# Mamba input projection of a decoder layer: batch by batch, with the softplus of batch 0 beside the projection of batch 1, and the convolution reading PSUM

## What is computed

```python
proj = hidden_states @ in_proj_w
x, z = jnp.split(proj, 2, axis=-1)
...
for k in range(K):
    xc = xc + conv_w[None, :, k:k + 1] * xp[:, :, k:k + Lq]
xc = jax.nn.silu(xc)
ssm_p = jnp.einsum('bdl,ed->ble', xc, x_proj_w)
dt_r = rmsnorm(ssm_p[..., :R], dt_ln_w)
...
dt = jnp.einsum('blr,dr->bdl', dt_r, dt_proj_w)
dt = jax.nn.softplus(dt + dt_bias[None, :, None])
...
ys = _selective_scan(xc, dt, A, Bm, Cm)
y = (ys + D_param[None, :, None] * xc) * jax.nn.silu(z)
```

## Time and profile before

| what | us |
|---|---|
| median of 3 runs | 3049.44 |
| lowest and highest run | 3047.0 and 3049.85 |
| span of the profiled execution | 3047.5 |
| VectorE, TensorE busy in it | 2393.1 and 2833.3 |
| first to last product of the input projection | 9 to 231.5 |
| softplus on VectorE | 236.9 to 318.3 |
| first scan step on VectorE | 318.24 |

### The profile page before, as it was taken

How to read it: one execution, slowest core, us unless ns; L and a number is a source line. 1 busy time by engine, 2 the same in 40 slices (tenths; PEclk the granted TensorE clock), 3 DMA queues, 4 the chain that set the end, 5 groups by cost and what they waited for, 6 DMA issues and landing times. The chain is left out here.

```text
span 3047.5 us, 35696 instructions
## 1 busy us (share of the span) xinstructions
PE 2833.3 (93%) x11958; PEld 2028.4 (67%) x11958; DVE 2393.1 (79%) x2168; ACT 1574.6 (52%) x2685; POOL 1712.8 (56%) x1035
## 2 busy tenths in 40 slices
PE   8997588888788889999999999999989999999997
PEld 7882244444222348888888888887768888887886
DVE  6558999999999977444777777765988888885677
ACT  4448555555665545213888888873433333334443
POOL 0003999999999953403888888861044444430034
PEclk9995799999999999999999999999989999999999
DMA  4228886666875645232111111215245555567654
GB/s 152 83 83 261 274 200 159 179 171 152 250 219 148 199 150 216 104 119 72 37 37 37 37 37 37 71 54 200 97 156 180 180 179 180 180 218 238 194 176 139
DMA packets 217641, 445.84 MB, mean 146 GB/s; under 512 B 33661, under 2 KB 47741, under 8 KB 215613
## 3 DMA queue, kind: packets, MB, share of 16 engines
q1 hardware_dynamic: 179742, 390.73, 41.1%
q10 hardware_dynamic: 37728, 52.96, 5.3%
HBM read 313.45 MB, written 130.15 MB: 146 GB/s over the span
## 5 line engine op out<-in xcount | busy, mean ns | idle before, releaser
L1927 POOL TENSOR_TENSOR at_p_lo<-at_p,at_p_hi 128x512 fp32r<-128x512 f32 x384 | 514.6, 1348 | 244.3 <-ACT at_p_hi L1820 236.5
L716 POOL TENSOR_TENSOR scan_dbx<-scan_u,scan_b_bc 128x1024 f32<-128x1024 f32 x256 | 596.1, 2359 | 0.0
L885 ACT ACTIVATE mamba_ps<-scan_dt,scan_a_neg 128x512 f32<-128x512 f32 (+1 forms) x512 | 332.0, 680 | 315.1 <-DVE scan_g L903 291.3
L914 DVE TENSOR_TENSOR_SCAN mamba_ps<-mamba_ps,scan_dbx 128x1024 f32<-128x1024 f32 x195 | 440.0, 2283 | 3.1 <-ACT mamba_ps L887 1.7
L1847 DVE TENSOR_REDUCE at_neg_max<-heads_ps 128x1 fp32r<-128x1536 f32 x128 | 224.9, 1757 | 134.4 <-PE heads_ps L1939 132.4
L108 PE MATMUL heads_ps<-ff_x_hi,ff_w_hi 128*128 128x512 f32 x784 | 310.0, 395 | 17.2 <-DVE ff_u L2572 6.4
L2812 POOL TENSOR_TENSOR ff_raw<-ff_raw,ff_scale 128x512 f32<-128x512 f32 x112 | 115.9, 1066 | 361.2 <-DMA ff_raw<-in_w 252.8
L109 PE MATMUL heads_ps<-ff_x_lo,ff_w_hi 128*128 128x512 f32 x784 | 308.1, 393 | 0.0
L110 PE MATMUL heads_ps<-ff_x_hi,ff_w_lo 128*128 128x512 f32 x784 | 308.1, 393 | 0.0
L1816 ACT ACTIVATE at_p<-heads_ps 128x512 f32<-128x512 f32 x384 | 228.2, 594 | 110.0 <-PE heads_ps L1963 95.8
L1820 ACT ACTIVATE at_p_hi<-at_p 128x512 fp32r<-128x512 f32 x384 | 242.8, 632 | 12.2
(11 more groups left out here) (306 smaller groups left out, 6906.8 us busy)
## 6 DMA issues: line engine op xcount, KB each, us to landing
scan_dt<-dt SPq DMA_DIRECT2D x120, 256.0 KB, 4.8
scan_u<-u SPq DMA_DIRECT2D x120, 256.0 KB, 7.6
ff_raw<-in_w SPq DMA_DIRECT2D x56, 512.0 KB, 4.6
ff_down_ar<-ac SPq DMA_DIRECT2D x98, 256.0 KB, 2.8
ff_down_hr<-hc SPq DMA_DIRECT2D x98, 256.0 KB, 2.7
ff_act_w<-in_w SPq DMA_DIRECT2D x14, 1024.0 KB, 7.6
hc<-ff_act_t SPq DMA_DIRECT2D x56, 256.0 KB, 6.2
ac<-ff_act_v SPq DMA_DIRECT2D x56, 256.0 KB, 5.9
```

The source lines that it names most:

```text
L716: nc.gpsimd.tensor_tensor(dbx[n % SL][:].rearrange("p (h l) -> p h l", h=2), u[it % 2][:, c:c + 2], b_bc[b][:, k // 2].unsqueeze(1).to_bro ...
L885: nc.scalar.activation(at[:, h * L + h:(h + 1) * L], dt[it % 2][:, c, h:L], ACT.Exp, scale=a_neg[:, it % IT, e:e + 1]).then_inc(a_ready, 1)
L914: nc.vector.tensor_tensor_scan(out[:], ps_a[n % SA], dbx[n % SL][:], 0.0, ALU.mult, ALU.add).then_inc(scanned, 1)
L1927: nc.gpsimd.tensor_tensor(p_lo[n % NSL][:], p[n % NSL][:], f32(p_hi[n % NSL][:]), ALU.subtract).then_inc(p_lo_done, 1)
```

## The change

The stage is reorganized; the rest of the program changes only in which z tiles it makes.

- Half tiles: step n = 0 to 31 is channel tile n % 16 of batch n // 16, 24 products into one PSUM bank, weights loaded again for batch 1. x is loaded, rounded and split per batch; batch 1's while batch 0 is projected. Steps 32 to 35 make z tiles 0 to 3 of batch 1. There are three weight buffers, and a weight's load waits for the end of the step that used its buffer.
- The convolution reads PSUM directly: four operations of 128x512 in place on `acc`, the shifted ones on a shorter range. The copy to xz is gone.
- The weight's remainder is made by GpSimd (`rest_w`), except the first.
- The remainder of `xpw` is made once for all tiles, after all seven small parameters have landed; ScalarE waits for these before it rounds the second weight.
- Softplus units i = 0 to 15 are two channel tiles of one batch. Units 0 to 7 (batch 0) are spread over steps 18 to 31 in groups of two, each group over four steps. Units 8 and 9 begin after step 33, the others after step 35.
- ee, ll, dd and uu have two buffers. The temporary is dd itself, in SBUF; the ramp is written to ll.
- SyncE issues the scan's first dt and u loads after step 35, ahead of the stores of units 8 to 15.
- The scan makes all 16 z tiles of batch 0 and tiles 4 to 15 of batch 1. Its gate steps begin at step 160 instead of 150 and follow each other every 10 steps instead of 12.

```diff
-    NT = 2 * IT - ZN
-    ND = 4
...
-    tail = Arena(nc, "in_tail")
...
+    NX = B * IT
+    NF = 2 * B
+    NT = NX + NF
+    NG = NX // 2
+    BG = NG // B
+    FIRST_GROUP = IT + 2
+    NW, NX3 = 3, 3
...
+    ee, ll, dd, uu = ([low(f"{n}{s}", [P, 2, L]) for s in range(2)] for n in ("ee", "ll", "dd", "uu"))
...
+    main_bank = [ps_all[:, n % 2] for n in range(NX + 2)] + [ps_all[:, 2], ps_all[:, 3]]
+    ps_xp, ps_ms = [ps_all[0:E, 6], ps_all[0:E, 7]], [ps_all[0:E, 4], ps_all[0:E, 6]]
+    ps_x = [ps_all[:, (4, 2)[i % 2]:(4, 2)[i % 2] + 2] for i in range(BG)]
+    ps_x += [ps_all[:, m:m + 2] for m in ((6, 4, 0)[i % 3] for i in range(BG))]
...
+        def load_w(n):
+            if n >= NW:
+                sp.wait_ge(main_done, n - NW + 1)
+            sp.dma_start(w[n % NW][:], d["w_in"][w_tile(n)]).then_inc(w_ld[n % NW], 16)
...
+        def store_pair(i):
+            sp.wait_ge(dt_done, i + 1)
+            sp.dma_start(d["dt"][2 * i:2 * i + 2].rearrange("i p l -> p i l"), dd[i % 2][:]).then_inc(dt_st[i % 2], 16)
+            sp.wait_ge(u_done, i + 1)
+            sp.dma_start(d["u"][2 * i:2 * i + 2].rearrange("i p l -> p i l"), uu[i % 2][:]).then_inc(u_st[i % 2], 16)
+
+        load_w(0)
+        load_x(0)
+        load_w(1)
...
+        load_w(2)
+        load_x(1)
+        sp.dma_start(dtw[:], d["dt_w"]).then_inc(dtw_ld, 16)
         scan.load_parameters(sp)
-        with sp.Fori(1, IT // 2) as j:
-            for s in range(2):
-                store_conv(2 * j + s - 2)
-                next_w(2 * j + s, s)
-        sp.wait_ge(w_lo_done, NT)
-        sp.dma_start(dtw[:], d["dt_w"]).then_inc(dtw_ld, 16)
+        pair = 0
+        for n in range(NX):
+            if n + NW < NT:
+                load_w(n + NW)
+            store_conv(n)
+            if n == IT:
+                store_bc(0)
+            if n >= FIRST_GROUP + 2 and (n - FIRST_GROUP) % 2 == 1:
+                store_pair(pair)
+                pair += 1
+        load_w(NT - 1)
+        for m in range(2):
+            store_gate(m)
...
+        store_bc(1)
...
+        scan.load_rows(sp, 0)
+        while pair < BG:
+            store_pair(pair)
+            pair += 1
+        for m in range(2, NF):
+            store_gate(m)
+        sp.wait_ge(main_done, NT)
         for s in range(2):
-            store_conv(IT - 2 + s)
+            sp.wait_ge(dt_st[s], 16)
+            sp.wait_ge(u_st[s], 16)
+        scan.load_dt(sp, 0)
+        scan.load_u(sp, 0)
+        scan.load_dt(sp, 1)
+        for i in range(BG, NG):
+            store_pair(i)
+        scan.load_u(sp, 1)
...
-        for i in range(IT):
-            sp.wait_ge(dt_done, i + 1)
-            sp.dma_start(dt[i], dd[i % ND][:]).then_inc(dt_st[i % ND], 16)
-            sp.wait_ge(u_done, i + 1)
-            sp.dma_start(u[i], uu[i % 2][:]).then_inc(u_st[i % 2], 16)
...
+                act.wait_ge(c_done, i - 1)
+                act.wait_ge(l_done, i - 1)
+            nc.scalar.activation(ee[i % 2][:], ps_x[i], ACT.Abs).then_inc(abs_done, 1)
...
+        act.wait_ge(par_ld, 16 * 7)
+        round_w(1)
+        nc.scalar.activation(xpw_hi[:], xpw[:], ACT.Copy).then_inc(xpw_hi_done, 1)
+        round_w(2)
+        for n in range(NX):
+            if n:
+                round_w(n + 2)
+            if 0 < n <= HT:
+                round_x(1, n - 1)
...
+            if group >= 0 and step == 0:
+                for i in range(2):
+                    logarithm(2 * group + i)
...
+            if group >= 0 and step == 0:
+                for i in range(2):
+                    exponentials(2 * group + i)
+        round_w(NX + 2)
+        gate(0)
+        squares(1)
+        root(1)
+        gate(1)
+        round_w(NX + 3)
+        for i in range(BG, NG, 2):
+            for n in range(2):
+                exponentials(i + n)
+            for n in range(2):
+                logarithm(i + n)
+            if i == BG:
+                for m in range(2, NF):
+                    gate(m)
 
...
-            nc.vector.tensor_tensor(w_lo[s][:], w[s][:], f32(w_hi[s][:]), ALU.subtract).then_inc(w_lo_done, 1)
...
+        def conv(n):
+            at, m = acc[n % 2], n % IT
+            dve.wait_ge(main_done, n + 1)
+            if n >= 2:
+                dve.wait_ge(xc_done, n - 1)
+            nc.vector.tensor_scalar(at[:], main_bank[n], cw[:, m, KC - 1:KC], cb[:, m:m + 1],
+                                    ALU.mult, ALU.add).then_inc(conv_step, 1)
+            for s in range(1, KC):
+                dve.wait_ge(conv_step, KC * n + s)
+                nc.vector.scalar_tensor_tensor(at[:, s:], main_bank[n][:, :L - s], cw[:, m, KC - 1 - s:KC - s], at[:, s:],
+                                               ALU.mult, ALU.add).then_inc(conv_step, 1)
...
+        def remainder(i):
+
+            dve.wait_ge(e_done, i + 1)
+            if i >= 2:
+                dve.wait_ge(dt_st[i % 2], 16 * (i // 2))
+                dve.wait_ge(u_done, i - 1)
+            nc.vector.tensor_scalar(dd[i % 2][:], ee[i % 2][:], 1.0, -1.0, ALU.add, ALU.add).then_inc(t_done, 1)
+            dve.wait_ge(t_done, i + 1)
+            nc.vector.tensor_tensor(dd[i % 2][:], ee[i % 2][:], dd[i % 2][:], ALU.subtract).then_inc(c_done, 1)
+
+        def ramp(i):
+            dve.wait_ge(l_done, i + 1)
+            nc.vector.scalar_tensor_tensor(ll[i % 2][:], ps_x[i], 0.0, ll[i % 2][:], ALU.max, ALU.add).then_inc(r_done, 1)
+
+        def total(i):
+            dve.wait_ge(r_done, i + 1)
+            dve.wait_ge(c_done, i + 1)
+            nc.vector.tensor_tensor(dd[i % 2][:], dd[i % 2][:], ll[i % 2][:], ALU.add).then_inc(dt_done, 1)
...
-                nc.vector.tensor_scalar(acc[s][:], xz[s][:, :, 0:L], cw[:, m, 0:1], cb[:, bass.ds(m, 1)],
-                                        ALU.mult, ALU.add).then_inc(conv_step, 1)
...
-            nc.vector.tensor_scalar(ps_t, ee[i % ND][:], 1.0, -1.0, ALU.add, ALU.add).then_inc(t_done, 1)
-            dve.wait_ge(l_done, i + 1)
-            if i >= ND:
...
-            nc.vector.scalar_tensor_tensor(dd[i % ND][:], ps_x[i % 3], 0.0, ll[i % ND][:],
-                                           ALU.max, ALU.add).then_inc(r_done, 1)
-            dve.wait_ge(t_done, i + 1)
-            nc.vector.tensor_tensor(ps_t, ee[i % ND][:], ps_t, ALU.subtract).then_inc(c_done, 1)
...
-            nc.vector.tensor_tensor(dd[i % ND][:], dd[i % ND][:], ps_t, ALU.add).then_inc(dt_done, 1)
...
+        for n in range(NX):
+            conv(n)
+            if n % IT:
...
+            group, step = divmod(n - FIRST_GROUP, 4)
+            i = 2 * group
+            if group >= 0 and step == 0:
+                remainder(i)
...
+            if group >= 0 and step == 1:
+                remainder(i + 1)
...
+            if group >= 0 and step == 1:
+                ramp(i)
+            if group >= 0 and step == 2:
+                ramp(i + 1)
+                total(i)
+            if group >= 0 and step == 3:
+                total(i + 1)
+        ramp(BG - 1)
+        normalize(1)
+        total(BG - 2)
+        total(BG - 1)
+        for i in range(BG, NG, 2):
+            for n in range(2):
+                remainder(i + n)
+            for n in range(2):
+                ramp(i + n)
+                total(i + n)
...
+        def rest_w(n):
+            pool.wait_ge(w_hi_done, n + 1)
+            nc.gpsimd.tensor_tensor(w_lo[n % NW][:], w[n % NW][:], f32(w_hi[n % NW][:]), ALU.subtract).then_inc(w_lo_done, 1)
...
+        for n in range(1, NX + 2):
+            rest_w(n + 2)
+            if n >= FIRST_GROUP + 2 and (n - FIRST_GROUP) % 2 == 0 and pair < BG:
+                product(pair)
+                pair += 1
+        for i in range(pair, NG):
+            if i == NG - 1:
...
+            product(i)
...
+            else:
+                pe.wait_ge(w_lo_done, n)
...
+            elif n >= 2:
+                pe.wait_ge(conv_step, KC * (n - 1))
...
+                last = three_passes(nc, main_bank[n], w_hi[n % NW][:, k], w_lo[n % NW][:, k], x_hi[b][:, k], x_lo[b][:, k],
+                                    k == 0, k == HT - 1)
...
+            pe.wait_ge(n_done, b + 1)
...
+            elif i >= 2:
+                pe.wait_ge(r_done, i - 1)
+            for n in range(2):
+                last = nc.tensor.matmul(ps_x[i][:, n], dtw[:, 2 * i % IT + n], dtr[:], start=True, stop=True)
             last.then_inc(dt_mm, 1)
 
-        pe.wait_ge(dtw_ld, 16)
...
+        for n in range(NX):
+            group, step = divmod(n - FIRST_GROUP, 4)
+            if group > 0 and step == 0:
...
+            elif n == FIRST_GROUP:
+                main(n, lambda: products(0), 1)
...
+            elif n >= 2:
+                xproj(n - 2)
+        main(NX)
+        xproj(NX - 2)
+        xproj(NX - 1)
+        main(NX + 1, lambda: mean_squares(1), 2)
+        for i in range(BG, BG + 2):
+            dt_product(i)
+        for n in range(NX + 2, NT):
+            main(n)
+        for i in range(BG + 2, NG):
             dt_product(i)
...
```

(7 more changed lines are left out.)

423 lines of the change are left out of this document (186 added, 237 removed).

## The result

The changed kernel takes 3073.3 us (median of 4 runs, 3071.5 to 3077.4) against 3048.7 for the kernel before (4 runs, 3047.0 to 3049.9). The ratio is 1.0081, interval 1.0067 to 1.0095. It is slower by 25 us; 3041 was forecast, and the range of 3020 to 3062 does not hold the result.

The account below looks back on a forecast made before the run. TensorE was taken to bound the projection, VectorE the softplus tail and scan. GpSimd's first scan product moves from 315.85 to 307.1: 3047.5 - 8.7 = 3038.8, plus 1.9, rounded to 3041 us; eight in ten from 3020 to 3062.

Parts of the forecast that it names:

- The idea's worth: Softplus ahead of the scan: eight of 16 units go beside batch 1's projection, 38.8 us the most to win.
- Start: Start of the program: main(1) begins at 17.6 us, 3.3 late, waiting for GpSimd's w_lo(1); bounds 0 to 6 us.
- Projection: Up to main(33): 888 products 200.9 us, dt products 14.2, VectorE in the way 7 (0 to 18); end at 245.2.
- Clock: Start of the program: TensorE's low clock covers 7 of main(0)'s 24 products, 0.43 us each, 3 us.
- the reciprocal: Projection: the first dt products wait for the reciprocal, 1 us.
- Collision: Batch 1's projection: VectorE operations with two SBUF inputs and GpSimd's wait for each other; 7 us (0 to 18).
- rival 2: Batch 1's projection: VectorE with its collisions becomes the bound; slower, 3068 us (3055 to 3085), chance 0.20.
- SyncE and the tail: Behind main(33): unit 8's store, behind 12 loads, lands at 273 and delays unit 10; groups of two units take 12.0 us.
- Edits at nothing: Scan: gate tiles in other order, later silu and gate products, and ps_a's order cost 0, within 3 us either way.

Follow-up runs that it names:

- the kernel without interleaving: Changed kernel with all 16 softplus units behind main(35) and four buffers for dt and u throughout: 3084.4 us.
- The earlier store: Changed kernel with SyncE storing the odd unit of each softplus group of batch 0 one half tile earlier: 3057.0 us.
- the filled kernel: Changed kernel plus 26, 12 and 16 products without use on TensorE where it stood idle: 3074.1 us.
- the kernel with the start's edits: Earlier odd-unit store, four buffers and loads on ScalarE (3045.1 us), plus w(1) rounded before the small-parameter wait and first dt products 4 steps later: 3037.9 us.

## Why the prediction was wrong

- **The idea's worth.** Not contradicted: 38.8 us at most was taken, and with and without interleaving the first scan step differs by 34.6 us. How near the two numbers are is partly luck, since the kernel without interleaving has stops of its own and the other waits 12.6 us for a store.
- **Start.** Right in kind. main(1) starts at 18.64 (17.6), behind GpSimd's w_lo(1) and ScalarE's wait for the last small parameter, which landed near 15.1 (14). Missed: TensorE's clock stands at half up to 23.5 us. 3.5 us late by main(17).
- **Projection: the step that failed.** "VectorE also gets in the way ... 7 us (0 to 18)" counted VectorE's work and its collisions, and put the wait for a buffer at nothing, without a reason. The step on SyncE was made for the tail alone. In the projection the same two buffers and the same queue stood in the code: remainder(3) comes right behind conv(23) on VectorE, and the store that it waits for comes behind store_conv(23) on SyncE, which waits for the silu of that very convolution. That closes a loop of silu, issue and landing. It cost VectorE 5.33, 3.65 and 3.55 us, one wait in each of three groups. It can be read from the two lists without any trace, with the landing of 3.8 us. The earlier store took away 16 us by this one edge.
- **Clock.** The sum's only low clock was at the very start. Each idle of 2 to 6 us on TensorE was followed by 6 to 13 us at half speed: 129.5 to 136, 191.3 to 204.4, 228 to 238.6, 260 to 266. Half of these 36 us is 18 us of TensorE's time, more than the idles themselves (2.06, 5.68, 2.37 and 3.59 us: 13.7). With the 3.5 us of the start, and less the 8 that the sum held for collisions and for the reciprocal, that makes 27 against the 24.8 found at main(33). In the filled kernel one such stretch, kept at the full clock, was 6.0 us shorter, near its half of 13.1; the next wait for a store took this back.
- **Collision.** Right in mechanism, and its size no longer decides. From 125 us on (min, median, max of each line's 16 instructions, ns):

```profile
L463 DVE TENSOR_TENSOR in_xc_lo<-xc,in_xc_hi x16: 681/684/2330, 131.5 to 259.1; 128x512 fp32r<-128x512 f32 x16
L486 DVE TENSOR_SCALAR in_dd<-in_ee x16: 680/692/2889, 143.2 to 331.5; 128x1024 f32<-128x1024 f32 x16
L488 DVE TENSOR_TENSOR in_dd<-in_ee,in_dd x16: 1224/1226/3253, 144.0 to 332.2; 128x1024 f32<-128x1024 f32 x16
L492 DVE SCALAR_TENSOR_TENSOR in_ll<-mamba_ps,in_ll x16: 1216/1218/1220, 151.2 to 335.8; 128x1024 f32<-128x1024 f32 x16
L497 DVE TENSOR_TENSOR in_dd<-in_dd,in_ll x16: 1212/1226/2339, 157.2 to 337.0; 128x1024 f32<-128x1024 f32 x16
```

  The line that reads PSUM never lengthens. In the projection the surplus is 8.7 us in all (5.7 on L463, 3.0 on L486), and once the stores are in time TensorE waits 4.9 us for xc_lo. So rival 2, the one that gave a loss of this size (3068), had the wrong mechanism: the loss came through a buffer, not through VectorE's work, and that its range of 3055 to 3085 holds the result is luck. With the stores in time main(33) still ends at 253.0, 7.8 us later than forecast; the 3.5 us of the start and the idle and low clock near 126 us (2.06 and half of 6.5) are 8.8, so what is left for VectorE's part is near the 7 us that were forecast.
- **SyncE and the tail.** Right in mechanism (store behind the loads, two buffers), but with one gap of two: the gap ahead of unit 10 was forecast at about 10 us and is 9.8, but the same gap ahead of unit 8, behind the 8 loads of rows, was overlooked: 11.9 us. VectorE was forecast to do units 8 and 9 in time that was free anyway; so unit 10 begins 35.8 us behind main(33) and not 27.8. From there to GpSimd's first scan product it is 1.6 us less than forecast. Groups take 11.65 us (12.0). The forecast of GpSimd's part in it holds too: without its product a group is 9.1 us.
- **Edits at nothing.** Right: the scan's new order of gate tiles costs nothing that can be measured (the span behind the first scan step is 2729.1 us against 2729.3).

What stays open is how much of the 16 us of the earlier store is the clock's and how much the wait's own: the windows give an estimate. The filling, which was to separate them, shows the clock's part in one stretch and not in the time, since the late stores stayed.

## What to carry to other kernels

Where a change cuts the number of buffers, write down for every reuse of one who empties it, and find that step in the emptying queue's own list: if what stands ahead of it depends on work of the waiting engine, the wait is as long as the whole loop, whatever the engines' loads. Count it in every stage that uses the buffers, not only in the one you look at. Price an idle of TensorE by the idle and the slow stretch that may follow it. And moving a block of transfers within one queue moved the wait with it in all three kernels that tried it; more buffers took away the waits that they bridged, and a second queue a part of one. Fewer transfers were not tried.

## What the runs showed of the hardware

- VectorE's operation with one SBUF input, L486 (128x1024), waits for GpSimd as well. Before the change no row showed this. VectorE and GpSimd in the changed kernel, near 172 us:

```profile
172.00 2.89 DVE L486 TENSOR_SCALAR in_dd<-in_ee 128x1024 f32<-128x1024 f32 x1
...
171.47 2.86 POOL L552 TENSOR_TENSOR in_uu<-in_dd,xc 128x1024 f32<-128x1024 f32 x1
```

  2.89 us against 0.69, and GpSimd's product 2.86 against 2.35. The rule cited in the prediction (the Trainium skill, GPSIMD Engine Reference, Key points) names operations in a 2-port perf mode beside those with two SBUF inputs. No row names the mode of L486. That it takes 0.69 us, where the same operation with its output in PSUM took 1.23 before (L457), fits the rule's first half and doesn't prove it.
- The wait lasts until GpSimd's instruction has ended (316.15 + 2.73 = 318.88, and 1.1 us behind that the subtraction is done):

```profile
316.71 3.25 DVE L488 TENSOR_TENSOR in_dd<-in_ee,in_dd 128x1024 f32<-128x1024 f32 x1
...
316.15 2.73 POOL L552 TENSOR_TENSOR in_uu<-in_dd,xc 128x1024 f32<-128x1024 f32 x1 [1.16 <-DVE in_dd L497]
```

  3.25 us against 1.23 is 2.0 us more, where the row of before showed 1.1 and the prediction took 2.2 as what could be had.
- TensorE's clock (granted clock 1.00 and 0.50) fell from 2.4 to 1.2 GHz behind idles of 2.1 to 5.7 us, and the stretches at 1.2 GHz were 6 to 13 us long; behind the same idle of 2.06 us it fell in one execution and not in another.
- Twenty loads of 256 KB held one queue for some 24 us (the estimate above), and issuing DMAs can itself hold an engine: four issues on ScalarE took 7.09 us while SyncE's stores and these loads ran at once, against 2.12 us for the same four in the kernel with the start's edits.
